# Attention and gated feed-forward on one core: the scaling of the probabilities moved from VectorE to ScalarE

## The reference

```python
xn = layernorm(x)                                  # x: 1024 tokens x 512
q = rmsnorm(xn @ Wq.T) * q_w                       # 32 heads of 128
k = rmsnorm(xn @ Wk.T) * k_w ; v = xn @ Wv.T       # 8 groups, each for 4 heads
attn = softmax(q @ k.T / sqrt(128) + slope * (key - query), causal)
s = (attn @ v) @ Wo.T
g = silu(ffn(xn))                                  # gated, dequantised weights, hidden 1792
out = x + s * g
```

## Time and profile before

| what | us |
|---|---|
| median of 3 runs | 1350.48 |
| lowest, highest | 1348.85, 1350.57 |
| profiled execution, own time | 1344.95 |
| its span | 1342.7 |
| attention, from the first scores to the last | about 42 to 1090 |
| feed-forward part | about 1090 to 1342 |

### The profile page before, as it was taken

How to read it: one execution, slowest core, us unless ns; L and a number is a source line. 1 busy time by engine, 2 the same in 40 slices (tenths; PEclk the granted TensorE clock), 3 DMA queues, 4 the chain that set the end, 5 groups by cost and what they waited for, 6 DMA issues and landing times. The chain is left out here.

```text
span 1342.7 us, 23192 instructions
## 1 busy us (share of the span) xinstructions
PE 1282.5 (96%) x7120; PEld 1100.7 (82%) x7120; DVE 968.2 (72%) x2067; ACT 649.5 (48%) x1420; POOL 743.5 (55%) x730
## 2 busy tenths in 40 slices
PE   5799999999999999999999999999999989999996
PEld 5678888888888888888888888888887878888884
DVE  5677877777777777777777777777888854555556
ACT  3555565555555555555555555555555523222222
POOL 3755575556555654664465446544565626555553
PEclk9899999999999999999999999999999999999998
DMA  3000000010000000000000001000020035454541
GB/s 119 17 17 16 32 16 17 17 32 16 16 16 32 16 16 16 32 16 16 16 32 16 16 16 32 16 16 16 16 63 25 0 100 167 128 134 128 131 106 63
DMA packets 29443, 57.42 MB, mean 43 GB/s; under 512 B 3648, under 2 KB 3648, under 8 KB 29248
## 3 DMA queue, kind: packets, MB, share of 16 engines
q1 hardware_dynamic: 29376, 56.68, 14.8%
HBM read 54.57 MB, written 2.10 MB: 42 GB/s over the span
## 5 line engine op out<-in xcount | busy, mean ns | idle before, releaser
L390 POOL TENSOR_TENSOR pb<-rel,coef 128x1024 f32<-128x1024 f32 (+7 forms) x256 | 299.3, 1187 | 100.6 <-PE T L845 92.1
L479 ACT ACTIVATE pb<-pb,low 128x1024 f32<-128x1024 f32 (+7 forms) x256 | 198.8, 777 | 188.9 <-DVE low L652 187.6
L469 ACT ACTIVATE pt_h<-T 128x512 fp32r<-128x512 f32 (+3 forms) x384 | 185.3, 486 | 127.8 <-PE T L845 125.8
L652 DVE CUSTOM_DVE_ANT_0 pb<-S,pb,ninv 128x1024 f32<-128x1024 f32 (+7 forms) x256 | 207.8, 812 | 45.5 <-PE S L867 39.0
L636 DVE TENSOR_TENSOR pt_l<-T,pt_h 128x512 fp32r<-128x512 f32 (+3 forms) x384 | 210.3, 550 | 41.2 <-ACT pt_h L469 40.2
L845 PE MATMUL T<-ident,pb 128*128 128x128 f32 x1152 | 190.1, 275 | 28.4 <-DVE pb L661 23.0
L845 PEld LDWEIGHTS T<-ident,pb 128*128 128x128 f32 x1152 | 140.9, 141 | 69.3 <-issue 25.6
L661 DVE TENSOR_SCALAR pb<-pb,rinv 128x1024 f32<-128x1024 f32 (+7 forms) x256 | 161.1, 629 | 9.0
L864 PE MATMUL S<-kT_h,q_h 128*128 128x512 f32 (+2 forms) x384 | 142.5, 371 | 2.7 <-DVE kT_l L724 2.7
L351 POOL TENSOR_TENSOR wo_l<-wo_in,wo_h 128x512 fp32r<-128x512 f32 x32 | 41.5, 1297 | 181.0 <-ACT wo_h L513 181.0
L883 PE MATMUL O<-pt_h,v_h 128*128 128x512 f32 (+2 forms) x384 | 140.7, 366 | 1.0 <-DVE pt_l L636 1.0
(11 more groups left out here) (138 smaller groups left out, 2988.2 us busy)
## 6 DMA issues: line engine op xcount, KB each, us to landing
wq_in<-in_wq SPq DMA_DIRECT2D x32, 256.0 KB, 2.7
wo_in<-in_wo SPq DMA_DIRECT2D x32, 256.0 KB, 2.6
stage<-in_wkv SPq DMA_DIRECT2D x8, 512.0 KB, 4.0
stage<-in_gate_w SPq DMA_DIRECT2D x14, 256.0 KB, 2.6
stage<-in_gate_z SPq DMA_DIRECT2D x14, 256.0 KB, 3.6
stage<-in_gate_s SPq DMA_DIRECT2D x14, 256.0 KB, 5.1
stage<-in_up_w SPq DMA_DIRECT2D x14, 256.0 KB, 5.2
stage<-in_up_z SPq DMA_DIRECT2D x14, 256.0 KB, 6.3
```

What stands on the lines that cost most here:

```text
L390: g_.tensor_tensor(pbuf(idx, t), rel[:, TOK - w:TOK], coef[:, t:t + 1].to_broadcast([P, w]), ALU.mult).then_inc(bias_ready, 1)
L469: a_.activation(pt_lot(pt_h, t, n), bank[:, 0:m * P].rearrange("p (k w) -> p k w", w=P), ACT.Copy).then_inc(tr_hi, 1)
L479: a_.activation(pbuf(idx, t), pbuf(idx, t), ACT.Exp, bias=low[:, idx:idx + 1], scale=-1.0, accum_out=rsum[:, idx:idx + 1]).then_inc(exps_r ...
L652: v_.tensor_tensor_reduce(out=pbuf(idx, t), in0=S[idx % 2][:, BASE[t]:BASE[t] + (t + 1) * P], in1=pbuf(idx, t), scale=ninv[:, t:t + 1], sc ...
```

## The change

VectorE's `normalise` becomes `invert`: it waits for the exponential and takes the reciprocal, and nothing else. ScalarE gets a `normalise`: it waits for `rinv_ready` and multiplies the buffer by the reciprocal, as a copy with a factor for each row, in place, and counts up `probs_ready`. It is written into ScalarE's order some instructions behind the exponential of the same tile. `invert` stands on VectorE where `normalise` stood. TensorE's and GpSimd's programs are the same.

```diff
@@ scalar
+        def normalise(h, idx):
+            t = TILES[idx]
+            act.wait_ge(rinv_ready, h * QT + (idx + 1))
+            a_.activation(pbuf(idx, t), pbuf(idx, t), ACT.Copy, scale=rinv[:, idx:idx + 1]).then_inc(probs_ready, 1)
...
         def group(g, kind):
             at = Places(kind, g)
+            if kind != "first":
+                normalise(g * PER - 1, 7)
             act.wait_ge(qk_ready, 1)
             act.wait_ge(kt_ready, g + 1)
             a_.activation(kT_h[:, :], S[0][:, :], ACT.Copy, scale=qk[:, 0:1]).then_inc(kt_hi, 1)
...
                     lots(h - 1, 1)
+                    if j > 0:
+                        normalise(h - 1, 7)
                     lots(h - 1, 0)
...
                 q_hi(at, f"qc0_{j}")
                 if j == 0:
                     exp(h, 0)
+                else:
+                    normalise(h, 0)
                 exp(h, 1)
+                if j == 0:
+                    normalise(h, 0)
                 if prev:
                     v_hi(at, f"v0_{j}", (j - 1) % PER)
+                normalise(h, 1)
                 lots(h, 7)
...
                     a_.activation(v_h[:, :, :], kv[:, :, HD:2 * HD], ACT.Copy).then_inc(v_hi_done, 1)
+                normalise(h, 2)
                 lot(h, 5, 0)
                 exp(h, 3)
                 lot(h, 5, 1)
+                normalise(h, 3)
                 if more:
                     q_hi(at, f"qc1_{(j + 1) % PER}")
                 lot(h, 4, 0)
                 exp(h, 4)
                 lot(h, 4, 1)
+                normalise(h, 4)
                 exp(h, 5)
                 if kind != "last":
                     k_squares(at, [f"kv{j}"], g + 1)
+                normalise(h, 5)
                 exp(h, 6)
                 lots(h, 3)
+                normalise(h, 6)
                 lots(h, 2)
...
         lots(HEADS - 1, 1)
+        normalise(HEADS - 1, 7)
         lots(HEADS - 1, 0)
@@ vector
-        def normalise(h, idx):
+        def invert(h, idx):
             dve.wait_ge(exps_ready, h * QT + (idx + 1))
             v_.reciprocal(rinv[:, idx:idx + 1], rsum[:, idx:idx + 1]).then_inc(rinv_ready, 1)
-            t = TILES[idx]
-            dve.wait_ge(rinv_ready, h * QT + (idx + 1))
-            v_.tensor_scalar(pbuf(idx, t), pbuf(idx, t), rinv[:, idx:idx + 1], None, ALU.mult
-                             ).then_inc(probs_ready, 1)
```

More of the change, by code:

```diff
@@ L721, in group @@
             if kind != "first":
-                normalise(g * PER - 1, 7)
+                invert(g * PER - 1, 7)
             dve.wait_ge(kt_hi, g + 1)
@@ L733, in group @@
                 if prev and j > 0:
-                    normalise(h - 1, 7)
+                    invert(h - 1, 7)
                 if j > 0:
@@ L740, in group @@
                 if j > 0:
-                    normalise(h, 0)
+                    invert(h, 0)
                     logits(h, 1)
@@ L748, in group @@
                 if j == 0:
-                    normalise(h, 0)
+                    invert(h, 0)
                 mean_sq(h, 0, part_no(h, "ss0"), T[0])
-                normalise(h, 1)
+                invert(h, 1)
                 if prev:
@@ L758, in group @@
                     project(at, f"w0_{j}", unit)
-                normalise(h, 2)
+                invert(h, 2)
                 lot(h, 6, 0)
@@ L765, in group @@
                 lot(h, 5, 0)
-                normalise(h, 3)
+                invert(h, 3)
                 lot(h, 5, 1)
@@ L773, in group @@
                 lot(h, 4, 0)
-                normalise(h, 4)
+                invert(h, 4)
                 if w and more:
@@ L778, in group @@
                 logits(h, 5)
-                normalise(h, 5)
+                invert(h, 5)
                 if not last:
@@ L787, in group @@
                 lots(h, 3)
-                normalise(h, 6)
+                invert(h, 6)
                 lots(h, 2)
@@ L803, in _ @@
         epi = Places("epi")
-        normalise(HEADS - 1, 7)
+        invert(HEADS - 1, 7)
         project(epi, "w1", 1)
```

## The result

| | before | after |
|---|---|---|
| median, us | 1350.21 (1348.85 to 1350.57) | 1391.57 (1387.60 to 1393.90) |
| profiled execution, own time | 1344.95 | 1393.90 |
| its span | 1342.7 | 1391.7 |
| mean granted clock of its TensorE | 0.992 | 0.985 |

The changed kernel is slower by a ratio of 1.0317 (95% interval 1.029 to 1.0343). The forecast was 1392 us.

A forecast was written before the change was run, and what follows sets the result against it. TensorE bounds the kernel, through whether its operands are ready. Plain heads 18.0, head 1 0.35, group starts 22.1, head 0 1.2, credits -3.2 and clock 3.0 make 41.5 us on 1350.5: 1392, range 1372 to 1412.

The forecast's parts named there:

- Margins bound it, not sums: Whole kernel: whether each TensorE step finds its operand ready counts; ScalarE at 94 of 132.6 us and VectorE at 82 don't bound.
- Cost of one scaling on ScalarE: Each ScalarE scaling: the exponential's duration, 1146 ns at 1024 wide and 939 at 768, less 0.1 us of overlap.
- The plain head, 0.75 us: Heads after a group's first: the idx 2 transposes wait 0.75 us for ScalarE's scaling; 24 heads lose 18.0 us.
- The walk down ScalarE's queue: Plain head from q_hi's end: scale 2 ends at 514.08, its transposes, wanted at 513.45, start at 514.20.
- The start of a group: First head of a group: delays reach 3.16 us through kT_h, scale 0 and scale 2; seven heads lose 22.1 us.
- VectorE's pause of its loop: Loop return: VectorE keeps its 2.6 us pause five times; no pause would give 1382 us, chance 0.13.
- The clock: Group starts: two more drops of the granted clock, 1.5 us each, 3.0 us in all, bounds 0 and 12.
- the 5.5 us that I added: Base of the forecast: the median shown, 1350.48 us, lies 5.5 above the profiled execution's 1344.95.
- Faster: Rival: idle ScalarE takes the scalings free of the port lock, up to 23 us of stalls go, 1336 us; chance 0.03.
- The clock's case: Rival: group-start stalls bring the clock down each time, +24 to +45 in place of 3, 1413 to 1434 us; chance 0.12.
- Shorter steps: Rival: every ScalarE step 10% shorter than the exponential's, plain heads lose 0.2 us, 1372 us; chance 0.05.

The follow-up runs named there:

- e8: The change with kT_h before scaling 7, scaling 0 before exp 1, tile 7's lots before scaling 1, scaling 2 between tile 6's lots: 1346.66 us, ratio 0.9992.
- e1: The change with the scaling of idx 2 back on VectorE: 1377.28 us, ratio 1.0217 to the kernel before.
- e3: The change with kT_h in front of scaling 7 at the start of a group: 1385.46 us, ratio 1.0284 to the kernel before.
- e7: The change with idx 2 left unscaled on both engines: 1364.32 us, ratio 1.0128 to the kernel before.
- e5: No engine scales the probabilities; VectorE still takes the reciprocals and the transposes wait for them: 1320.80 us, ratio 0.9805 to the kernel before.
- e6: The change with only idx 3 to 7 scaled on ScalarE and kT_h before scaling 7: 1336.29 us, ratio 0.9912 to the kernel before.
- e2: The change with scaling 0 before exp 1 also in the first head of a group: 1379.22 us, ratio 1.0235 to the kernel before.
- e4: The change with only idx 3 to 6 scaled on ScalarE, the rest on VectorE: 1345.84 us, ratio 0.9983 to the kernel before.

## Why the prediction was right, and where it was not

- **Margins bound it, not sums: right.** ScalarE has 0.4 of the span to spare and the kernel lost 3.2%. e8 shows it: the same sums, about 45 us less. The sums themselves were 92 us a group on ScalarE for the 94 forecast, and 85 on VectorE for 82.
- **Cost of one scaling on ScalarE: right.** I took the exponential's duration (1146 ns at 1024, 939 at 768), measured 1147 and 926.
- **The plain head, 0.75 us: right, a little small.** In head 14 the transposes of tile 5 are 0.72 us later behind those of idx 0 and TensorE stands idle for 0.60 us before them, for the scaling, as named; in the heads before and behind it they are 0.85 and 0.86 us later. The walk down ScalarE's queue held to 0.1 us at every step that the rows show. The period of a plain head grew by 0.8 to 1.0 us: the trace has the remaining 0.1 us in small parts behind that wait, and no second wait.
- **The start of a group: right.** Waits of 1.89 us at idx 0 (about 1.9), 1.54 at idx 2 (about 1.7), 0.61 for kT_l (0.7). From the idx 2 transposes of head 15 to those of head 16 it takes 4.7 us more than before. One fall of the clock, 1.6, is in that, and what is left is about 3.1 where the walk said 3.16.
- **VectorE's pause of its loop: right.** It stays with 198 instructions a group, five times, and ScalarE with 196 has none. What decides which loop pauses is not shown by the runs.
- **The clock: the mechanism right, the size not.** The term of 3.0 us, "I count two more drops", was mis-sized. In the profiled execution there are five more in the repeated groups, all behind the wait for idx 0, and one more in the first group. A fall costs 1.4 to 1.6 us, as heads of one run with and without it show (before, e1, e3, e7), so the term should have been about 9. My bound of 12 (one more in each group) held it.
- **The total.** Against the profiled execution, on which the sum was made, the forecast was 1386.4 and 1393.9 was measured: 49.0 us in place of 41.5. About 6 of the 7.5 us are the clock's term. The rest is the 0.1 to 0.2 us a plain head, less some 1.5 us that the first and last groups lost less than forecast. That the median came out at 1391.57 against 1392 is luck: the 5.5 us that I added to go from the profiled execution to the median happened to make up for most of those 7.5. The 17 runs of the kernel before that stand beside e5 to e8 lie in two clumps: 1343.5 to 1345.1 us at a mean granted clock of 0.991 to 0.993 (and one of 1347.1 at 0.991), and 1347.9 to 1350.3 at 0.986 to 0.989. The profiled execution (0.992) is like the first, the median shown like the second. So the 5.5 us were clock falls of the kernel before, and the changed kernel, which has its falls in the profiled execution already, did not need them added again. That the clumps are counts of falls is worked out from the mean clocks; only one execution of each kernel was traced.
- **The rivals.** Faster: the walk spoke against it, and the run bears that out for the change. e8 (even) and e6 (0.9% faster) show how near it was, since it only needed other places. The clock's case came in part: six more falls, not 16 to 32. Its upper end was also summed wrongly, since 48 us in place of 3 make 1437, not 1434. Shorter steps are out by the 1147 ns at 1024.

## What to carry to other kernels

When work moves to an idle engine that runs in order, don't ask how busy it is. Take every consumer's margin (from the end of the step to the first instruction that reads it) and walk the receiving queue down from the last thing that its engine has to wait for: work may go where the margin is larger than all that now stands before it, and each instruction put in also delays what stands behind it. Move only the steps with room and put them behind the urgent ones: the same edit was 3% slower, even, or 0.9% faster by nothing but which steps moved and where they stood. And compare a profiled execution with the median by its mean granted clock too, before one is used as the base of the other.

## What was not expected of the hardware

- One and the same wait does or does not bring the granted clock down. Behind the 1.9 us before the idx 0 transposes it fell in six of six repeated groups with the change, in four of six in e3, in five of six in e7 and in one of six in e1; with that wait at 0.94 us (e2, e8) in none of six. In the kernel before a wait of 2.14 us brought it down once in five times in the profiled execution, and in e4 a wait of 2.1 us did the same. One fall cost 1.4 to 1.6 us in a group of 140. What decides whether it falls is not shown.
- A scaling of 768 columns on VectorE took 1.08 us beside a GpSimd product, against 0.62 to 0.64 us alone, and the GpSimd instruction behind the product took 1.33 us against 1.00. The stretching depends on how two queues happen to line up: taking one step back to VectorE (e1) brought it in where the kernel before had none.
